# A hybrid-mixer and routed-expert kernel: the last batch's input in the first one's place, the first weight splits in one go, register loads moved into TensorE's idle time, and helper work moved to GpSimd

## The chip, the cores and the metric

The program runs on one core of one Trainium2 chip. The metric is device time in microseconds (us) for one execution; the kernel before was timed three times. The engines are named as in the profile: PE is TensorE (PEld its weight loads), DVE is VectorE, ACT is ScalarE, POOL is GpSimd, SP is SyncE, which issues most of the DMAs. A "q" behind an engine's name (PEldq, ACTq, DVEq, SPq) is that engine's instruction sequencer.

## What is computed

```python
x = L0_attn_x                                   # (4 batches, 512 tokens, 512 features)
h = _layernorm(x) * (1 + ca) + sa               # ca, sa, ga, cb, sb, gb come from silu(c) @ wmod
x = x + ga * _L0_attn_ref(h, ...)               # mixer: causal depthwise conv, B, C, delta products, a scan
h = _layernorm(x) * (1 + cb) + sb
...
logits = x_flat @ w_router.T                    # 2 experts, the token goes to the better one
top_idx = jnp.argmax(probs, axis=-1)
h = jnp.einsum('nd,ehd->enh', x_flat, w_fc)     # 512 -> 2048
a = jnp.square(jnp.where(h >= 0, h, 0.5 * h))
expert_out = jnp.einsum('enh,edh->end', a, w_proj)
out = jnp.einsum('end,en->nd', expert_out, mask * top_weight[None, :])
x = x + gb * out
```

## The kernel before

**Stages.** The program has two large stages. In the first, the mixer, the four batches (`b` = 0 to 3) go one after the other through layernorm, transposes, convolution, scan and output product, and give `res`, the rows after the mixer. For each batch the router's margin is worked out (`margin_products`, `newton2`, `margins`), the tokens of the two experts are counted (`prefix` on PE, `ranks` on DVE), and each block of 128 tokens is permuted on PE (`permuted_block`) and written into the sorted array `XSfull` at a row number that is known only at run time (`place`, from the front for one expert and from the back for the other). In the second stage, the experts, the sorted rows are 17 blocks of 128, in five units of 4, 4, 4, 3 and 2 blocks, and the hidden width is cut into 8 blocks (`hb`). For each unit PE makes the first product (`first_fc` for units 0 and 1 of block 0, else `fc`), DVE and ACT make the square, and PE makes the second product (`proj`).

**High and low parts.** All expert products are made in three passes of a reduced format. A tile is split into a high part (a rounded copy, made by ACT: `Whi`, `XShi`, `ahi`) and a low part (full minus high, made by DVE or POOL: `Wlo`, `XSlo`, `alo`). The weights' two tiles have 8 chunks of 512 columns: chunks 0 to 3 serve the first product, chunks 4 to 7 the second.

**Order of the work.** Every engine's order is written out by hand, and engines wait for each other by semaphores. Around the change it is this. When batch 3 has its mask, PE makes `prefix(3)`, loads four run-time row numbers and expert picks (`load_unit(0)`, `load_unit(1)`), makes the high-high pass of unit 0 (`first_fc(0, (0,))`), the four permuted blocks of batch 3, the other two passes of unit 0, the three of unit 1, seven more register loads, and then `proj(0, 0, 0)`, the first product of the second kind. From there on PE has work until almost the end. DVE makes `ranks(3)`, `permutations(3)`, `low_rows(0)` (the low part of unit 0's rows), `lows(range(4))` (the low weights 0 to 3), `assign_rest` (which rows units 2 to 4 hold), `low_rows(1)`, and then for unit 0 `place_from_back` of blocks 0 and 1, `twice`, `place_from_back` of blocks 2 and 3, and `low`. ACT makes `place(2, ...)`, `high_rows(0)`, `high_rows(1)`, `place(3, (0, 1))`, the high weights 4 to 7 (`split_first(range(4, CH))`) and the first unit's job.

**Memory.** The fourth batch's input `x3` has a place of its own, in the bytes of the high weights 4 to 7; these weights can only be split when batch 3's residual has been read. The inputs of batches 0 to 2 lie in a ring of three places, `x_in`, in the bytes of `XShi`. SP loads `x3` when the third modulation row is done (`s_mm`), and behind it in its queue stand the store of the scaled router rows (`wd_dram`), their four broadcast loads `bc`, which `margin_products(0)` reads, and the router's sums.

**Register loads.** `value_load` reads one number from memory into a register of the engine. In the trace it is three instructions of the sequencer: `TENSOR_LOAD`, `FUSED_REGOPS`, `SEQ_ASSERT`.

Of the kernel before, what the change touches and what calls it, by code (L numbers as in the profile page):

```python
# [104 lines left out]
def build(nc, x, cT, wmod, wx, win, wout, conv_w, conv_b, A_log, Dvec, router_rows, wffn, out):  # L105
    with ExitStack() as ctx:
# [296 lines left out]
        s_early = sem("first_units_assigned")  # L403
        s_unit = sem("units_assigned")
# [30 lines left out]
        def _(sp):  # L435
# [3 lines left out]
            def load_x(b):  # L439
                sp.dma_start(x_in[:, b] if b < XRING else x3[:, :, :], x[b]).then_inc(s_x[b], 16)  # L440
# [22 lines left out]
            sp.wait_ge(s_mm, 4)  # L463
# [49 lines left out]
        def _(pool):  # L513
# [52 lines left out]

            def low(hb, c):
                pool.wait_ge(s_whi, CH * hb + c + 1)
                pool.tensor_tensor(Wlo[:, hb % 2, c, :], raw[:, c, :], Whi[:, hb % 2, c, :].bitcast(F32),  # L569
                                   ALU.subtract).then_inc(s_wlo, 1)  # L570

            for b in range(NB):
# [3 lines left out]
                positions(b)  # L576
                if b == NB - 1:

                    pool.wait_ge(s_wlo, CH // 2)
# [80 lines left out]
        def _(act):  # L660
# [96 lines left out]

            def place(b, js=range(TJ)):
# [107 lines left out]
            def high_rows(u):  # L866
                start_row = act.value_load(startI[0:1, u:u + 1], min_val=0, max_val=ROWS - P * UNITS[u])
                for k in range(KT):
                    act.activation(XShi[:, k, bass.ds(start_row, P * UNITS[u])], XSfull[:, k, bass.ds(start_row, P * UNITS[u])],
                                   ACT.Copy).then_inc(s_xhi, 1)  # L870


            act.wait_ge(s_early, 2)
            act.wait_ge(s_e0, KT * TJ * (NB - 1))
# [48 lines left out]
            for u in range(NU):  # L923
                if u == 0:
                    job(0, 0, 0, ((place, (NB - 1, (2, 3))),))
# [3 lines left out]
                else:  # L929
                    job(0, 0, u, ((high_rows, (u + 1,)),) if u + 1 < NU else ())  # L930
# [22 lines left out]
        def _(pe):  # L953
# [114 lines left out]

            def prefix(b):
# [5 lines left out]
            def permuted_block(b, j):  # L1075
# [16 lines left out]
                mm.then_inc(s_pz, 1)  # L1092

# [22 lines left out]
            for b in range(NB):  # L1116
# [45 lines left out]
                if b == 0:  # L1162
                    delta_product(2)
                prefix(b)
# [108 lines left out]
            start_row, pick = [], []  # L1273

            def load_unit(u):
                start_row.append(pe.value_load(startI[0:1, u:u + 1], min_val=0, max_val=ROWS - P * UNITS[u]))
                pick.append(pe.value_load(pickI[0:1, u:u + 1], min_val=0, max_val=2))


            pe.wait_ge(s_early, 2)  # L1280
            load_unit(0)
            load_unit(1)
# [4 lines left out]
            for j in range(TJ):  # L1287
                permuted_block(NB - 1, j)
            first_fc(0, (1, 2))
# [25 lines left out]
        def _(dve):  # L1315
# [166 lines left out]
            def prepare_rest():  # L1482


                own.link(dve.tensor_scalar(rows_in_front[:, :], ends[:, 1:2], float(P), None, ALU.mult))
                own.mark(dve.tensor_scalar(basis[:, 0:NU - 2], basis[:, 0:NU - 2], rows_in_front[:, 0:1], None, ALU.add))
                own.link(dve.tensor_scalar(limits[:, :], blkF[:, 0:LEFT], rows_in_front[:, 0:1], None, ALU.add))
# [316 lines left out]
```

## Time and profile before

| | |
|---|---|
| timed runs | 545.67, 542.83, 544.35 us; median 544.35 us |
| the profiled execution | 547.68 us, its span 545.9 us |
| granted TensorE clock, mean over the span | 0.958 |
| busy: PE, DVE, ACT, POOL | 92%, 63%, 48%, 29% |
| first matmul of `proj(0, 0, 0)` | at 167.32 us of the span |

The span runs from the first to the last instruction. The chain of work that ended last is followed back from the last instruction. A granted clock of 1.00 is 2.4 GHz, 0.50 is 1.2 GHz. Times in rows are microseconds from the start of the span, followed by the length of the group.

### The profile page before, as it was taken

Reading aid. Unit: us, or ns where it says so; the run is one execution under the profiler, and the core shown is the slowest. Engines: PE = TensorE matmul, PEld = TensorE weight load, DVE = VectorE, ACT = ScalarE, POOL = GpSimd, SP = SyncE. Lnnn points to the kernel's source line nnn. Section 1 sums busy time; section 2 is a strip of 40 time slices with the busy share of each in tenths; the row PEclk is TensorE's granted clock in tenths of the full one; section 3 lists DMA queues with packets and bytes.
Section 4 is the critical chain, followed back from the end, with each engine's and each line's share of the span. In section 5 each row is a group of like instructions: output and inputs, shape, how many; then the busy total and the mean of one; then the engine's idle time right before and its main releaser. Section 6 shows DMA issues by size and latency. Waiting matters only on the chain.

```text
span 545.9 us, 7958 instructions
## 1 busy us (share of the span) xinstructions
PE 502.0 (92%) x2408; PEld 392.8 (72%) x2408; DVE 345.7 (63%) x730; ACT 259.4 (48%) x524; POOL 158.4 (29%) x204
## 2 busy tenths in 40 slices
PE   7899789987397999999999999999999999999990
PEld 1464365736276888898888888888888888988880
DVE  4579999699998575454445354545454534668781
ACT  1774295956785633443443354344345334433220
POOL 1100021122243510330150033034004304868673
PEclk9899969998697999999999999999999999999995
DMA  8931242220051004130022022002102300468692
GB/s 294 424 133 57 103 152 77 79 77 2 1 162 72 4 3 156 30 126 2 1 79 79 1 78 80 1 1 94 64 1 78 118 1 6 117 112 182 78 167 98
DMA packets 15730, 46.31 MB, mean 85 GB/s; under 512 B 5223, under 2 KB 5223, under 8 KB 12344
## 3 DMA queue, kind: packets, MB, share of 16 engines
q1 hardware_dynamic: 10600, 34.71, 17.9%
q0 software_dynamic: 5072, 10.79, 9.6%
q8 instruction: 41, 0.67, 0.5%
q14 instruction: 17, 0.14, 0.1%
HBM read 37.30 MB, written 8.71 MB: 84 GB/s over the span
## 4 chain that ended last, share of the span: by engine, by line
PE 75%; DVE 13%; ACT 4%; issue 3%; DMA 1%; ACTq 1%; POOL 1%; DVEq 0%; SPq 0%; POOLq 0%
PE bank L1232 34%; PE bank L1201 32%; DVE xc L1359 3%; ACT XSfull L777 2%; DVE st L1404 1%; DVE st L1341 1%; DMA x_in<-x 1%; PE bank L1030 1%; PE bank L1038 1%; DVE res L1397 1%; PE bank L1063 1%; PE bank L1006 1%; DVE eabs L1421 1%; PE bank L1067 1%; DVE hs L1387 1%
## 5 line engine op out<-in xcount | busy, mean ns | idle before, releaser
L569 POOL TENSOR_TENSOR Wlo<-raw,Whi (+1 forms) x60 | 76.6, 1307 | 228.0 <-ACT Whi L921 219.9
L1656 DVE TENSOR_TENSOR acc<-acc,bank 128x512 f32<-128x512 f32 x110 | 74.8, 687 | 57.2 <-PE bank L1232 57.2
L1232 PE MATMUL bank<-Whi,ahi 128*128 128x512 f32 x268 | 105.5, 394 | 4.3 <-DVE alo L1646 4.3
L1640 DVE TENSOR_TENSOR twice_h<-twice_h,bank 128x512 f32<-128x512 f32 (+2 forms) x80 | 48.2, 605 | 95.6 <-ACT twice_h L892 95.5
L1201 PE MATMUL bank<-XShi,Wlo 128*128 x304 | 108.1, 356 | 0.0
L1201 PE MATMUL bank<-XSlo,Whi 128*128 x304 | 108.0, 355 | 0.0
L1201 PE MATMUL bank<-XShi,Whi 128*128 x304 | 108.0, 355 | 0.0
L1232 PE MATMUL bank<-Wlo,ahi 128*128 128x512 f32 x268 | 105.5, 394 | 0.0
L1232 PE MATMUL bank<-Whi,alo 128*128 128x512 f32 x268 | 105.3, 393 | 0.0
L901 ACT ACTIVATE ahi<-twice_h 128x512 fp32r<-128x512 f32 (+2 forms) x78 | 44.6, 572 | 120.0 <-PE bank L1232 119.9
L892 ACT ACTIVATE twice_h<-bank 128x512 f32<-128x512 f32 (+2 forms) x78 | 41.4, 533 | 86.9 <-PE bank L1201 76.2
L1201 PEld LDWEIGHTS bank<-XSlo,Whi 128*128 128x128 f32 x304 | 57.3, 189 | 7.5
L1201 PEld LDWEIGHTS bank<-XShi,Whi 128*128 128x128 f32 x304 | 57.3, 189 | 7.5
L1201 PEld LDWEIGHTS bank<-XShi,Wlo 128*128 128x128 f32 x304 | 57.3, 188 | 6.8
L1232 PEld LDWEIGHTS bank<-Whi,ahi 128*128 128x128 f32 x268 | 51.0, 190 | 14.9 <-issue 4.7
L1232 PEld LDWEIGHTS bank<-Whi,alo 128*128 128x128 f32 x268 | 50.9, 190 | 10.8
L1232 PEld LDWEIGHTS bank<-Wlo,ahi 128*128 128x128 f32 x268 | 50.9, 190 | 10.2
L1646 DVE TENSOR_TENSOR alo<-a_full,ahi 128x512 fp32r<-128x512 f32 (+2 forms) x78 | 45.4, 612 | 0.0
L902 ACT ACTIVATE a_full<-twice_h 128x512 f32<-128x512 f32 (+2 forms) x78 | 43.3, 556 | 0.0
L1359 DVE SCALAR_TENSOR_TENSOR xc<-hT,cw,xc 128x512 f32<-128x512 f32 x48 | 33.6, 742 | 2.5 <-ACT xc L703 2.2
L777 ACT ACTIVATE XSfull<-bank,cols 128x128 f32 (+1 forms) x64 | 24.1, 460 | 20.0 <-PE bank L1091 17.7
L921 ACT ACTIVATE Whi<-raw 128x512 fp32r<-128x512 f32 x56 | 30.5, 616 | 0.0
(201 smaller groups left out, 570.1 us busy)
## 6 DMA issues: line engine op xcount, KB each, us to landing
raw<-wffn SPq DMA_DIRECT2D x16, 1024.0 KB, 5.1
wm<-wmod SPq DMA_DIRECT2D x6, 1024.0 KB, 12.8
out<-res SPq DMA_DIRECT2D x4, 1024.0 KB, 4.5
x_in<-x SPq DMA_DIRECT2D x3, 1024.0 KB, 12.4
ga_bc<-ga_rows SPq DMA_DIRECT2D x4, 256.0 KB, 3.7
x<-x SPq DMA_DIRECT2D x1, 1024.0 KB, 5.1
bc<-router_rows_scaled SPq DMA_DIRECT2D x4, 256.0 KB, 3.5
wx_sb<-wx SPq DMA_DIRECT2D x1, 514.0 KB, 8.6
```

The costliest lines, as they stand in the source:

```text
L569: pool.tensor_tensor(Wlo[:, hb % 2, c, :], raw[:, c, :], Whi[:, hb % 2, c, :].bitcast(F32), ALU.subtract).then_inc(s_wlo, 1)
L777: act.activation(XSfull[:, k, bass.ds(first, P)], place_bank[b][j][:, P * k:P * k + P], ACT.Identity, bias=cols[:, 4, k, b:b + 1], scale=c ...
L892: act.activation(twice_h[:, m, 0:w], hP[(par + u) % 2][m][:, 0:w], ACT.Relu).then_inc(s_relu[m], 1)
L901: act.activation(ahi[:, m, 0:w], twice_h[:, m, 0:w], ACT.Square, scale=0.5).then_inc(s_ah[m], 1)
L902: act.activation(a_full[:, m, 0:w], twice_h[:, m, 0:w], ACT.Square, scale=0.5).then_inc(s_af[m], 1)
L921: act.activation(Whi[:, 1 - par, c, :], raw[:, c, :], ACT.Copy).then_inc(s_whi, 1)
L1201: mm = pe.matmul(hP[(par + u) % 2][m][:, c0:c1], W[wp][:, par, 2 * e + k // 2, o:o + P], XS[xp][:, k, bass.ds(start_row[u] + c0, c1 - c0)] ...
L1232: mm = pe.matmul(yP[bank_of[s]][:, :], ahl[ap][:, m, P * s:P * s + P], W[wp][:, par, 4 + 2 * experts[s] + m, :], start=(m == 0 and n == 0) ...
L1359: ins = dve.scalar_tensor_tensor(xc[:, b % 2, k, :], hT[b % 2][:, k, tap:tap + L], cw[:, k, tap:tap + 1], xc[:, b % 2, k, :], ALU.mult, AL ...
L1640: dve.tensor_tensor(twice_h[:, m, 0:w], twice_h[:, m, 0:w], hP[(par + u) % 2][m][:, 0:w], ALU.add).then_inc(s_q2[m], 1)
L1646: dve.tensor_tensor(alo[:, m, 0:w], a_full[:, m, 0:w], ahi[:, m, 0:w].bitcast(F32), ALU.subtract).then_inc(s_al2[m], 1)
L1656: dve.tensor_tensor(acc[:, n, :], acc[:, n, :], yP[s][:, :], ALU.add).then_inc(s_yu, 1)
```

## The change

The fourth batch is loaded into ring place 0 after batch 0's residual has been read. ACT splits all eight first weights in one go before `place(2, ...)`. The low weights 0 to 3 go from DVE to POOL, ahead of POOL's scatter DMAs of batch 2; the low weights 4 to 7 stay on POOL but wait for `low_rows(1)`. `prepare_rest` (four small operations) goes from DVE to POOL. PE loads the registers of units 0 and 1 ahead of `prefix(3)`, followed by three matmuls whose result is not used (`keep_rate`), and those of units 2 to 4 ahead of the second and third pass of unit 0. ACT and DVE load row numbers earlier. ACT makes the rank guess `guess2(3)` after block 2 of batch 2 instead of after block 1, and three blocks of batch 3 instead of two ahead of unit 0's job. The top weights and the count of batch 3 move from unit 0 to unit 1 on DVE.

```diff
-        x3 = at("x3", [P, TJ, DM], F32, o_whi + ZB)
-
         def x_row(b, j):
-            return x_in[:, b, j, :] if b < XRING else x3[:, j, :]
+            return x_in[:, b % XRING, j, :]
...
-            sp.wait_ge(s_mm, 4)
+            sp.wait_ge(s_x2, TJ)
             load_x(3)
             sp.wait_ge(s_wdr, 1)
             sp.dma_start(wd_dram, wd_row[:, :]).then_inc(s_wds, 16)
...
+            def prepare_rest():
+                pool.wait_ge(s_early, 2)
+                own.link(pool.tensor_scalar(rows_in_front[:, :], ends[:, 1:2], float(P), None, ALU.mult))
...
+                pool.tensor_scalar(limits[:, :], limits[:, :], -1.0, float(TOK), ALU.mult, ALU.add).then_inc(s_limits, 1)
...
+                if b == NB - 2:
+                    prepare_rest()
+
+                    pool.wait_ge(s_x2, TJ * (NB - 1) + 1)
+                    pool.wait_ge(s_pb, 2 * NB)
+                    pool.wait_ge(s_cv, KT * NB)
+                    for c in range(CH // 2):
+                        low(0, c)
                 if b == NB - 1:
 
+                    pool.wait_ge(s_xlo, KT * 2)
                     pool.wait_ge(s_wlo, CH // 2)
                     for c in range(CH // 2, CH):
                         low(0, c)
...
-            split_first(range(4))
-            place(2, (0, 1))
+            split_first(range(CH))
+            place(2, (0, 1, 2))
             guess2(3)
-            place(2, (2, 3))
...
             act.wait_ge(s_early, 2)
+            first_rows = [first_row(u) for u in range(2)]
+            place(2, (3,))
...
-            high_rows(0)
-            high_rows(1)
+            act.wait_ge(s_x2, TJ * NB)
+            high_rows(0, first_rows[0])
+            high_rows(1, first_rows[1])
             margin_exp(3)
-            place(NB - 1, (0, 1))
-
-            act.wait_ge(s_x2, TJ * NB)
-            split_first(range(4, CH))
+            place(NB - 1, (0, 1, 2))
...
+            def keep_rate(b, count):
+
+                pe.wait_ge(s_q, TJ * b + 2)
+                pe.wait_ge(s_x2, TJ * (b + 1))
+                for n in range(count):
+                    pe.matmul(pO[1][:, :], ident[:, :], wout_sb[:, :], start=True, stop=True)
...
+                if b == NB - 1:
+
+                    pe.wait_ge(s_early, 2)
+                    load_unit(0)
+                    load_unit(1)
+                    keep_rate(b, 3)
                 prefix(b)
...
             first_fc(0, (0,))
             for j in range(TJ):
                 permuted_block(NB - 1, j)
-            first_fc(0, (1, 2))
-
-            pe.wait_ge(s_x2, TJ * NB)
-            first_fc(1, (0, 1, 2))
             pe.wait_ge(s_unit, 2)
             for u in range(2, NU):
                 load_unit(u)
             pick.append(pe.value_load(pickI[0:1, NU:NU + 1], min_val=0, max_val=2))
+            first_fc(0, (1, 2))
+
+            pe.wait_ge(s_x2, TJ * NB)
+            first_fc(1, (0, 1, 2))
...
-                    if b == NB - 1:
-                        prepare_rest()
...
+            first_rows = [first_row(u) for u in range(2)]
             ranks(NB - 1)
             permutations(NB - 1)
-            low_rows(0)
-            lows(range(4))
             assign_rest()
-            low_rows(1)
+            dve.wait_ge(s_off, NB)
+            low_rows(0, first_rows[0])
+            first = [first_place(j) for j in range(2)]
+            low_rows(1, first_rows[1])
+            first += [first_place(j) for j in range(2, TJ)]
...
-                if u == 0:
+                if u == 1:
                     own.link(dve.tensor_scalar(n0f[:, :], run[:, :], -1.0, float(TOK), ALU.mult, ALU.add))
```

On PE, between the permuted blocks of batch 2 (`bank<-perm,z`) and the prefix counts of batch 3 (`bank<-m,before` and `bank<-m,ones`), the kernel before has nothing, and the register loads of units 0 and 1 follow the counts (`startI` holds row numbers, `pickI` expert picks):

```order
L1091 MATMUL bank<-perm,z_71 128x128 x8
L1072 MATMUL bank<-m_140,before 128x4
L1073 MATMUL bank<-m_140,ones 128x4
L1276 TENSOR_LOAD startI
L1276 ISA x2
L1277 TENSOR_LOAD pickI
L1277 ISA x2
```

In the changed kernel the same place reads:

```order
L1118 MATMUL bank<-perm,z_71 128x128 x8
L1124 TENSOR_LOAD startI
L1124 ISA x2
L1125 TENSOR_LOAD pickI
L1125 ISA x2
L1124 TENSOR_LOAD startI
L1124 ISA x2
L1125 TENSOR_LOAD pickI
L1125 ISA x2
L1094 MATMUL bank<-wout_sb,ident 128x512 x3
L1099 MATMUL bank<-m_139,before 128x4
L1100 MATMUL bank<-m_139,ones 128x4
```

The four loads and three new matmuls now stand ahead of the counts, and the first pass of unit 0 follows the counts directly.

Further on in PE's order, the end of unit 1's passes, the seven later loads (the last five rows of them here) and the first row of `proj(0, 0, 0)` stood like this before:

```order
L1180 MATMUL bank<-XShi,Wlo 128x512 x8
L1188 UNCONDITIONAL_BRANCH
L1276 TENSOR_LOAD startI
L1276 ISA x2
L1277 TENSOR_LOAD pickI
L1277 ISA x2
```

and in the changed kernel the seven loads begin right behind the permuted blocks of batch 3 and end in front of unit 0's second pass (`bank<-XSlo,Whi`), of which this is the end:

```order
L1124 TENSOR_LOAD startI
L1124 ISA x2
L1125 TENSOR_LOAD pickI
L1125 ISA x2
L1321 TENSOR_LOAD pickI
L1321 ISA x2
L1225 COMPARE_AND_BRANCH
L1219 ISA
L1219 MATMUL bank<-XSlo,Whi 128x512
```

On DVE, from the permutation masks of batch 3 on (`perm`), the kernel before makes the low rows of unit 0 and the low weights ahead of the assignment of the later units (`begun`, `change`, `assignment`):

```order
L1454 TENSOR_SCALAR perm<-colidx,place_col 128x128 x4
L1619 TENSOR_LOAD startI
L1619 ISA x2
L1622 ISA
L1622 TENSOR_TENSOR XSlo<-XSfull,XShi 128x512
L1622 ISA
L1622 TENSOR_TENSOR XSlo<-XSfull,XShi 128x512
L1622 ISA
L1622 TENSOR_TENSOR XSlo<-XSfull,XShi 128x512
L1622 ISA
L1622 TENSOR_TENSOR XSlo<-XSfull,XShi 128x512
L1527 TENSOR_TENSOR Wlo<-raw,Whi 128x512 x4
```

In the changed kernel:

```order
L1483 TENSOR_SCALAR perm<-colidx,place_col 128x128 x4
L1514 TENSOR_SCALAR begun<-limits,run 128x8
L1515 TENSOR_TENSOR change<-change,begun 128x56
L1517 TENSOR_REDUCE assignment<-change 128x7
L1518 TENSOR_TENSOR startI<-assignment,basis 128x3
L1519 TENSOR_TENSOR pickI<-assignment,basis 128x4
L1639 ISA
L1639 TENSOR_TENSOR XSlo<-XSfull,XShi 128x512
```

The assignment now comes first, the register load is gone from this place, and the four low weights are gone from DVE.

## Rows read from the trace of the kernel before

**Rows 1.** Chain that ended last, in order of time: start, length, what.
```profile
167.32 8.16 PE bank L1232 x24
175.48 5.44 PE bank L1201 x24
```

**Rows 2.** Timeline of PE from batch 3's counts to the first second product.
```profile
145.19 0.59 PE L1072 MATMUL bank<-m,before 128*128 128x4 f32 x2 [5.19 <-DVE m L1435]
...
148.50 3.70 PE L1180 MATMUL bank<-XShi,Whi 128*128 x8 [2.30 <-ACT XShi L869]
152.04 1.91 PE L1091 MATMUL bank<-perm,z 128*128 128x128 f32 x16
153.70 2.07 PE L1180 MATMUL bank<-XSlo,Whi 128*128 x8
...
167.32 0.80 PE L1232 MATMUL bank<-Whi,ahi 128*128 128x512 f32 x1 [4.29 <-DVE alo L1646]
```

**Rows 3.** Timeline of DVE in the same stretch.
```profile
148.83 2.50 DVE L1622 TENSOR_TENSOR XSlo<-XSfull,XShi  x4
151.25 2.49 DVE L1527 TENSOR_TENSOR Wlo<-raw,Whi 128x512 fp32r<-128x512 f32 x4
...
155.18 3.60 DVE L1622 TENSOR_TENSOR XSlo<-XSfull,XShi  x4 [0.54 <-issue]
158.70 1.35 DVE L1633 TENSOR_SCALAR XSfull<-bank,cols 128x128 f32 x4
...
161.56 1.27 DVE L1640 TENSOR_TENSOR twice_h<-twice_h,bank 128x512 f32<-128x512 f32 x2
...
165.61 1.28 DVE L1646 TENSOR_TENSOR alo<-a_full,ahi 128x512 fp32r<-128x512 f32 x2
```

**Rows 4.** Timeline of POOL: the low weights 4 to 7.
```profile
156.64 5.80 POOL L569 TENSOR_TENSOR Wlo<-raw,Whi 128x512 fp32r<-128x512 f32 x4 [8.01 <-ACT Whi L756]
```

**Rows 5.** Timeline of ACT in the same stretch.
```profile
147.05 4.27 ACT L869 ACTIVATE XShi<-XSfull  x8 [0.80 <-ACT XSfull L781]
...
154.47 1.51 ACT L777 ACTIVATE XSfull<-bank,cols 128x128 f32 x4 [0.20 <-ACT XSfull L777]
155.85 2.20 ACT L756 ACTIVATE Whi<-raw 128x512 fp32r<-128x512 f32 x4
157.94 1.09 ACT L892 ACTIVATE twice_h<-bank 128x512 f32<-128x512 f32 x2
```

**Rows 6.** PE's sequencer by line: durations ns min/median/max, first and last start.
```profile
L1276 PEldq TENSOR_LOAD <-startI x2: 297/362/427, 159.2 to 160.6; - x2
...
L1296 PEldq SEQ_ASSERT  x1: 18/18/18, 163.8 to 163.8; - x1
...
L1089 PEldq EVENT_SEMAPHORE  x2: 51/51/51, 150.0 to 150.2; - x2
```

**Rows 7.** One stretch: us, busy PE, PEld, DVE, ACT, POOL, then granted clock, DMA share, GB/s.
```profile
140.00:142.00 2.00, 0.00 (x0) 0.00 (x0) 1.68 (x8) 1.18 (x6) 0.00 (x0) 0.93 0.00 0
```

**Rows 8.** Timeline of PE: three matmuls of full format, 512 columns, two records each.
```profile
61.49 2.74 PE L1048 MATMUL bank<-xc,win_sb 128*128 128x512 f32 x6
```

**Rows 9.** Timeline of SP and DVE around the router rows' broadcast.
```profile
56.48 0.68 DVE L1397 TENSOR_TENSOR res<-bank,x_in 128x512 f32<-128x512 f32 x1
...
61.24 1.74 SPq L470 DMA_DIRECT2D bc<-router_rows_scaled  x4
...
64.35 2.46 DVE L1341 BATCH_NORM_STATS2 st<-x 128x6 f32<-128x512 f32 x4
...
67.48 0.69 DVE L1421 CUSTOM_DVE_ANT_0 eabs<-res,bc 128x512 f32<-128x512 f32 x1
```

**Rows 10.** DMA issues on the page: size, median us from issue to landing.
```profile
x_in<-x SPq DMA_DIRECT2D x3, 1024.0 KB, 12.4
...
x<-x SPq DMA_DIRECT2D x1, 1024.0 KB, 5.1
...
bc<-router_rows_scaled SPq DMA_DIRECT2D x4, 256.0 KB, 3.5
```

More of the change, by code:

```diff
@@ L403, in build @@
         s_early = sem("first_units_assigned")
+        s_limits = sem("limits_ready")
         s_unit = sem("units_assigned")
@@ L439, in load_x @@
             def load_x(b):
-                sp.dma_start(x_in[:, b] if b < XRING else x3[:, :, :], x[b]).then_inc(s_x[b], 16)
+                sp.dma_start(x_in[:, b % XRING], x[b]).then_inc(s_x[b], 16)
             sp.dma_start(c_sb[:, :], cT).then_inc(s_c, 16)
@@ L756, in split_first, with first_row, high_rows @@
                     act.activation(Whi[:, 0, c, :], raw[:, c, :], ACT.Copy).then_inc(s_whi, 1)
+            def first_row(u):
+                return act.value_load(startI[0:1, u:u + 1], min_val=0, max_val=ROWS - P * UNITS[u])
+            def high_rows(u, start_row):
+                for k in range(KT):
+                    act.activation(XShi[:, k, bass.ds(start_row, P * UNITS[u])], XSfull[:, k, bass.ds(start_row, P * UNITS[u])],
+                                   ACT.Copy).then_inc(s_xhi, 1)
             def place(b, js=range(TJ)):
@@ L924, in _ @@
                 if u == 0:
-                    job(0, 0, 0, ((place, (NB - 1, (2, 3))),))
+                    job(0, 0, 0, ((place, (NB - 1, (3,))),))
                     act.wait_ge(s_e0, KT * NBLK)
@@ L929, in _ @@
                 else:
-                    job(0, 0, u, ((high_rows, (u + 1,)),) if u + 1 < NU else ())
+                    job(0, 0, u, ((lambda n: high_rows(n, first_row(n)), (u + 1,)),) if u + 1 < NU else ())
                 if u == 1:
@@ L1092, in permuted_block, with load_unit @@
                 mm.then_inc(s_pz, 1)
+            start_row, pick = [], []
+            def load_unit(u):
+                start_row.append(pe.value_load(startI[0:1, u:u + 1], min_val=0, max_val=ROWS - P * UNITS[u]))
+                pick.append(pe.value_load(pickI[0:1, u:u + 1], min_val=0, max_val=2))
             pe.wait_ge(s_const, 9)
@@ L1480, in assign_first @@
                 dve.tensor_copy(startI[:, 0:2], startf[:, :]).then_inc(s_early, 1)
[L1482 to L1487, printed above, removed]
-                own.link(dve.tensor_scalar(limits[:, :], limits[:, :], -1.0, float(TOK), ALU.mult, ALU.add))
             def assign_rest():
                 dve.wait_ge(s_change, CHANGES)
+                dve.wait_ge(s_limits, 1)
                 own.link(dve.tensor_scalar(begun[:, :], limits[:, :], run[:, 0:1], None, ALU.is_gt))
@@ L1617, in _, with first_row, low_rows @@
                 margins(b)
-            def low_rows(u):
-                start_row = dve.value_load(startI[0:1, u:u + 1], min_val=0, max_val=ROWS - P * UNITS[u])
+            def first_row(u):
+                return dve.value_load(startI[0:1, u:u + 1], min_val=0, max_val=ROWS - P * UNITS[u])
+            def low_rows(u, start_row):
                 for k in range(KT):
@@ L1623, in low_rows, with first_place, place_from_back @@
                                       XShi[:, k, bass.ds(start_row, P * UNITS[u])].bitcast(F32), ALU.subtract).then_inc(s_xlo, 1)
-            def place_from_back(j):
+            def first_place(j):
+                return dve.value_load(offI[0:1, (NB - 1) % 2, j:j + 1], min_val=0, max_val=P * (TJ * (NB - 1) + j))
+            def place_from_back(j, first):
                 b = NB - 1
                 n = TJ * b + j
-                first = dve.value_load(offI[0:1, b % 2, j:j + 1], min_val=0, max_val=P * n)
                 dve.wait_ge(s_e0, KT * (n + 1))
@@ L1711, in _ @@
                 if u == 0:
-                    place_from_back(0)
-                    place_from_back(1)
+                    place_from_back(0, first[0])
+                    place_from_back(1, first[1])
                 twice(0, 0, u)
                 if u == 0:
-                    place_from_back(2)
-                    place_from_back(3)
+                    place_from_back(2, first[2])
+                    place_from_back(3, first[3])
                 elif u + 1 < NU:
-                    low_rows(u + 1)
+                    if u == 1:
+                        dve.wait_ge(s_unit, 2)
+                    low_rows(u + 1, first_row(u + 1))
                 if u > 0:
```

20 lines of the change are left out of this document (4 added, 16 removed).

## Prediction

> **What bounds the kernel now.** I read the chain of waits first. It is mixed up to 167.32 us of the span and is PE alone from there: the second and first products of the experts follow each other without a gap [rows 1] until the last few microseconds. The change adds and removes no matmul behind that point. So its worth is the moment at which `proj(0, 0, 0)` starts, and the rate at which PE then runs.
>
> Next I read the timeline of PE in front of that moment. The last pass of unit 1 was done at about 163.0, and PE then sat idle for 4.29 us, until DVE had made `alo` [rows 2]. In the idle time the granted clock fell: the first 24 matmuls of `proj` took 8.16 us, the next 24, of the same size, 5.44 us [rows 1]. The reader is to see two separate losses there, 4.29 us of idle time and 2.72 us of slow clock.
>
> Then I followed back what `alo` waited for, on DVE and ACT. DVE is busy almost without a gap from 148.83: low rows 2.50, low weights 2.49, assignment, low rows 3.60, two blocks from the back from 158.70, `twice` 1.27, two more blocks, `alo` [rows 3]. The 3.60 is the same work as the 2.50; it ran long while POOL made its low weights, from 156.64 [rows 3, 4]. ACT had unit 0's `h` waiting while it split the weights 4 to 7 (2.20 us), and made the first half of the square at 157.94 [rows 5]. DVE is thus the engine that sets `proj`'s start, with ACT close behind.
>
> **The change, part by part.**
>
> *DVE.* The four low weights (2.49) leave it. The register load in front of `low_rows(1)` (0.54 of idle time) is hidden, and the 1.10 by which `low_rows(1)` ran long is avoided, since POOL now waits for it [rows 3]. Counting nothing for `prepare_rest`, the masks are done at 148.8 as before. The assignment takes about 0.9 (from the end of the low weights at 153.74 to 155.18, less the 0.54), so 149.8. Two times 2.50 of low rows end at 154.8, where they ended at 158.78 before. Two blocks of 1.35 with a gap of 0.2 end at 157.7. DVE is then some 4 us earlier, and waits for ACT.
>
> *PE, the loads.* This is the part that costs. Seven loads took from 159.2 to 163.8, so 4.6 us, 0.66 each [rows 6], and before they lay beside unit 1's matmuls and the idle time. Now they stand in front of unit 0's second pass. PE's sequencer had passed the waits of the permuted blocks at 150.2 [rows 6], well ahead of the matmuls, which ended at about 153.9 [rows 2]. Its condition, the assignment, is met at 149.8. So the loads run from 150.3 to 154.9. With 0.4 for the branch (as from the end of `alo`, 166.89, to 167.32) the second pass starts at 155.3 instead of 153.70 [rows 2]: 1.6 us later. Unit 0's two remaining passes take 3.7 (from 153.70 to 157.4 before, and 16/24 of 5.44), so its `h` is complete at 159.0.
>
> *ACT.* The weight split leaves this place and goes to a wait ahead of `place(2, ...)`; it was on the way of `twice_h` only through its 2.20 us, of which one more block of 1.51 takes the place [rows 5]. From the complete `h` at 159.0: the last half of the first operation, 0.55, ends at 159.65.
>
> *The sum.* From 159.65 on DVE: half of `twice` 0.65, two blocks 2.9 with their gap, `alo` 1.28 [rows 3], branch 0.42: 164.9. ACT has one block (1.7 with its gap) and four squares of 0.56 ahead of the second `alo`, which gives 163.6, within that. So `proj` starts at about 165.0 instead of 167.32: **2.3 us** earlier. Unit 1's three passes (5.44) run from 159.0 to 164.5. PE's idle time ahead of `proj` shrinks from 4.29 to 0.5 us, and with it goes the reason for the slow clock: **2.7 us** [rows 1]. Together 5.0 us.
>
> *Against it.* PE is done with the permuted blocks at 152.2 to 153.9 and now idles until 155.3, up to 3.1 us. Before, the clock was at 0.93 in the mean of a stretch in which PE did nothing, so it fell inside it, some 2 us after the last matmul of that place [rows 7]. If it falls in the new gap too, unit 0's passes run at 1.2 GHz for a while. The bounds are 0 and 3.7 us (all 16 matmuls at half rate); a pass of eight at the lower level took 3.70 against 2.07 [rows 2], so one slow pass costs 1.6. I take 0.8, the middle of none and one.
>
> The Trainium skill speaks on this against the change, in "TensorE: Matmul & The Clock Gate", Part 4: it says that a transpose does not count as PE being busy in the way a matmul does, so the 1.9 us of permuted blocks ahead of the gap would not hold the clock up. The trace agrees as far as it goes, since the blocks of batch 2 did not keep the clock from falling. By that rule one slow pass, 1.6, would be taken in full, and the sum would be 3.4 us.
>
> *`keep_rate` and the first loads.* Four loads (2.6 by the rate of the seven) and three matmuls now stand ahead of `prefix(3)`, in PE's 5.19 us of idle time before 145.19 [rows 2]. PE's last matmul ahead of it ended at 140.0; the sequencer is a little ahead, so I put the loads' end at 142.1. Three matmuls of full format took 2.74 us at full rate [rows 8], so 2.7, or 5.4 at half. At full rate they end at 144.8, ahead of the mask; at half rate at 147.5, and the counts, which DVE used at about 147.2 before, come up to 1.5 us late. DVE has 4 us to spare later, but the loads' condition moves too. I take 0 and keep 1.5. What the matmuls may bring, a first pass at full rate (1.6 us), hides behind the seven loads.
>
> *ACT's loads.* Three in a row ahead of the last block of batch 2, about 1.9; `high_rows(0)` then starts close to its 147.05 [rows 5]. No gain, and up to 0.5 late; PE's first pass is covered by the loads. `guess2(3)` moves behind a block of 1.5 and its copy; DVE's four margin products give it about that time.
>
> *The fourth input.* It is issued after batch 0's last residual (56.48 + 0.68), 57.2 [rows 9], and lands 5.1 us later [rows 10], 62.3; its first reader stands at 64.35 [rows 9]. Behind it in SP's queue are the router rows' store and the four `bc` loads, issued at 61.24. If the store ends with the input, `bc` is issued at 62.4 instead, the last of the four at 63.7, and lands 3.5 later, at 67.2. Its reader stands at 67.48 [rows 9, 10]. Cost 0, with a slack that is nearly gone.
>
> "DMA: Bandwidth & Descriptors" of the Trainium skill, Queues, rings and completion order, says that each DMA engine takes a queue's descriptors in ring order. No stretch of this trace shows a small store behind a large load; by the rule it waits for the load, which the case above already assumes.
>
> *POOL.* Its four low weights (5.80 [rows 4]) run from about 134.6 to 140.4; batch 2's scatters come after and end near 145.5, when the mask arrives. The second four run from 154.8 to 160.6, and `proj` needs them at 165. Nothing here is on the path.
>
> **The rivals.** First, the clock takes the gain: it falls in the gap of the loads and again ahead of `proj`, or the counts come late by 1.5. Then `proj` starts 0 to 2 us earlier and partly at half rate: 0.3 to 2.6 us gained, 541.8 to 544.0. For it speaks the 3.1 us gap; against it, that unit 1's passes run right into `proj`. The change then does not do what it says for TensorE's waits: one is removed and one made. Chance 0.22.
>
> Second, more is gained: the seven loads overlap with the permuted blocks so that the second pass still starts at 153.7. That gives 1.6 more, 6.6 us, 537.8. Against it stand the 4.6 us. Chance 0.12.
>
> Third, slower: the fourth input lands late. The loads into `x_in` had a median of 12.4 us to landing, in a full queue [rows 10]. With 12.4 it would land at 69.6, `bc` at 74.5 instead of 67.2, and DVE would stand 7.0 us from 67.48, in a stretch where the counts on PE wait for DVE. With the 4.2 us gained elsewhere that is 547.1. It decides against the change from a landing later than about 9 us after issue. DMA has nothing else to do at that time, so 0.10, other losses included.
>
> **How the numbers follow.** The forecast (0.56) is 5.0 less 0.8, 4.2 us. The profiled execution took 547.68, so its counterpart is 543.5; the median of the three runs is 544.35, and I forecast 540.1, its own range 538.6 to 541.5. The runs shown differ by 2.8 us, so 0.5% (2.7 us) is about what a measurement can tell from no change. To hold 8 in 10 the range goes up into the first rival and down to the second: 537.0 to 544.6. Faster by over 0.5%: the forecast, the second rival, nothing of the first: 0.68. Within: 0.22. Slower: 0.10.
>
> **What would show it.** In the changed kernel: seven register loads on PE's sequencer ending near 155, unit 0's second pass right after them, DVE's second low rows at 2.5 us and over by 155; `proj(0, 0, 0)` near 165 with an idle time under 1 us and 24 matmuls in 5.4 us; the input's landing near 62.3 and no wait of DVE for `bc`. I am wrong if PE's idle time only moves ahead of unit 0's second pass and brings the slow clock with it, or if anything before 145 comes late.

## The result, and the profile after

The changed kernel took 552.84 us in the median of 4 runs (551.69 to 553.85), against 543.85 for the kernel before in the same comparison: a ratio of 1.0147, 95% interval 1.0115 to 1.018. It is slower, where 540.1 was forecast. The profiled execution took 553.41, with a span of 551.6.

The chain that ended last, of the changed kernel, two stretches: start, length, what (L1271 is `proj`, L1240 `fc`). A `...` in a view marks rows left out.
```profile
167.02 5.78 PE bank L1271 x24
172.80 5.44 PE bank L1240 x24
...
189.99 2.90 issue
192.89 0.69 DVE alo L1665
193.58 0.42 issue
194.00 7.65 PE bank L1271 x24
```

These answer to [rows 1]. `proj(0, 0, 0)` starts at 167.02, 0.3 earlier, and its 24 matmuls take 5.78 where they took 8.16: 2.4 gained, as the prediction's second term said. But 27 us later there is a break that [rows 1] do not have. The loss is there: TensorE stands still, and then runs 24 matmuls in 7.65 instead of 5.44 (its granted clock from 194 to 198 is 0.50). The rows around it, by engine:

Timelines of POOL, DVE, ACT and PE of the changed kernel, 176 to 194 us (L604 and L608 are the scatters, L578 the low weights, L1665 `alo`).
```profile
176.15 1.02 POOL L604 DMA_INDIRECT sorted_rows<-meta,posI  x1 [16.80 <-issue]
...
181.36 1.11 POOL L608 DMA_INDIRECT sorted_rows<-gap,gapI  x1 [0.30 <-issue]
182.49 9.92 POOL L578 TENSOR_TENSOR Wlo<-raw,Whi  x8
...
184.33 9.24 DVE L1665 TENSOR_TENSOR alo<-a_full,ahi 128x512 fp32r<-128x512 f32 x2
...
184.84 2.18 ACT L941 ACTIVATE Whi<-raw 128x512 fp32r<-128x512 f32 x4
...
194.00 0.80 PE L1271 MATMUL bank<-Whi,ahi 128*128 128x512 f32 x1 [6.13 <-DVE alo L1665]
```

The two `alo` instructions of unit 2 took 9.24 us together, where those of unit 0 took 1.28 [rows 3]. One of them alone lasted 8.6 us. It ended at 192.97, 0.6 after POOL's eight low weights (192.41), so it ran only when they were through. The view of the tile `alo` (count, ns min/median/max):
```profile
L1665 DVE TENSOR_TENSOR alo<-a_full,ahi x2: 679/4660/8642, 184.3 to 192.9; 128x512 fp32r<-128x512 f32 x2
```

The two spans add up: 0.3 and 2.4 gained, 6.1 of idle time and 2.2 of slow clock lost, which is 5.6 us; the spans differ by 5.7 (551.6 less 545.9). The medians differ by more, since the profiled execution of before (547.68) was itself 3.8 above its median.

Why the eight run in one piece shows in POOL's first row: the scatters of batch 3 start at 176.15. In the kernel before they started at 168.26, and the low weights of block 1 came in two fours, at 177.66 and 188.52, with the `alo` of unit 2 (187.00) between them. Timelines of POOL and DVE of the kernel before (L569 are the low weights, L1646 `alo`).
```profile
168.26 1.02 POOL L586 DMA_INDIRECT sorted_rows<-meta,posI  x1 [5.82 <-issue]
...
177.66 5.05 POOL L569 TENSOR_TENSOR Wlo<-raw,Whi  x4 [3.16 <-ACT Whi L921]
188.52 5.24 POOL L569 TENSOR_TENSOR Wlo<-raw,Whi  x4 [5.81 <-ACT Whi L921]
```
```profile
187.00 1.33 DVE L1646 TENSOR_TENSOR alo<-a_full,ahi 128x512 fp32r<-128x512 f32 x2
```
There POOL waited 5.81 us ahead of the second four, for ACT's second half of the high weights. In the changed kernel POOL comes so late that this half is being made (184.84) while it works on the first four, and it goes straight on.

The scatters wait for the weights of batch 3 and the count (`n0f`, `gapI`, `top_weight(3)`), and the change moves these on VectorE from unit 0 to unit 1, the last line of the diff.

The transition itself, for [rows 2] and [rows 3]. Timelines of PE and DVE of the changed kernel.
```profile
140.76 5.46 PE L1094 MATMUL bank<-wout_sb,ident 128*128 128x512 f32 x6 [3.12 <-DVE q L1450]
...
149.69 1.91 PE L1118 MATMUL bank<-perm,z 128*128 128x128 f32 x16
154.36 3.77 PE L1219 MATMUL bank<-XSlo,Whi 128*128 x8 [2.76 <-DVE XSlo L1639]
```
```profile
142.19 0.17 DVE L1464 TENSOR_SCALAR m<-lg 128x4 f32<-128x4 f32 x1
...
146.91 0.16 DVE L1470 TENSOR_TENSOR place_col<-cand,bank 128x4 f32<-128x4 f32 x1 [2.36 <-PE bank L1100]
...
149.38 4.91 DVE L1639 TENSOR_TENSOR XSlo<-XSfull,XShi  x8
...
160.51 0.69 DVE L1659 TENSOR_TENSOR twice_h<-twice_h,bank 128x512 f32<-128x512 f32 x1 [3.35 <-ACT twice_h L912]
```
The three matmuls of `keep_rate` ran at half rate (5.46 where [rows 8] have 2.74, granted clock 0.50 from 142 to 146), held the counts back, and VectorE stood 2.36 us. The low rows run undisturbed (4.91 for both units). TensorE stood 2.76 us ahead of unit 0's second pass, whose eight matmuls took 3.77.

### The profile page after: what moved, and what is told of

The parts are those of the page before. It is cut to its first block, busy times and chain, and to the rows that moved or that the text cites. A ratio compares the mean times of both kernels' runs of the same rounds, so it can differ in the third digit from the quotient of the medians.

```text
span 551.6 us, 7975 instructions
## 1 busy us (share of the span) xinstructions
PE 506.8 (92%) x2414; PEld 394.1 (71%) x2414; DVE 349.1 (63%) x722; ACT 260.0 (47%) x524; POOL 163.8 (30%) x212
## 4 chain that ended last, share of the span: by engine, by line
PE 72%; DVE 18%; issue 4%; ACT 2%; DMA 1%; DVEq 1%; POOL 1%; SPq 0%; ACTq 0%; POOLq 0%
PE bank L1271 34%; PE bank L1240 32%; DVE xc L1388 4%; PE bank L1219 2%; DVE st L1433 2%; DVE res L1426 2%; DVE st L1370 1%; DMA x_in<-x 1%; DVE eabs L1450 1%; PE bank L1094 1%; DVE hs L1416 1%; PE bank L1050 1%; PE bank L1068 1%; PE bank L1058 1%; PE bank L981 1%
## 5 line engine op out<-in xcount | busy, mean ns | idle before, releaser
L578 POOL TENSOR_TENSOR Wlo<-raw,Whi (+1 forms) x64 | 80.4, 1292 | 224.0 <-ACT Whi L941 217.9
L1271 PE MATMUL bank<-Whi,ahi 128*128 128x512 f32 x268 | 105.5, 394 | 6.5 <-DVE alo L1665 6.5
L1240 PE MATMUL bank<-XShi,Wlo 128*128 x304 | 108.1, 356 | 0.0
L1240 PE MATMUL bank<-XSlo,Whi 128*128 x304 | 108.1, 355 | 0.0
L1240 PE MATMUL bank<-XShi,Whi 128*128 x304 | 108.1, 355 | 0.0
L1271 PE MATMUL bank<-Wlo,ahi 128*128 128x512 f32 x268 | 105.3, 393 | 0.0
L1271 PE MATMUL bank<-Whi,alo 128*128 128x512 f32 x268 | 105.2, 392 | 0.0
L1271 PEld LDWEIGHTS bank<-Whi,ahi 128*128 128x128 f32 x268 | 50.9, 190 | 17.4 <-issue 7.2
L1240 PEld LDWEIGHTS bank<-XShi,Whi 128*128 128x128 f32 x304 | 57.3, 189 | 7.5
L1240 PEld LDWEIGHTS bank<-XSlo,Whi 128*128 128x128 f32 x304 | 57.3, 189 | 7.5
L1240 PEld LDWEIGHTS bank<-XShi,Wlo 128*128 128x128 f32 x304 | 57.3, 189 | 6.9
L1271 PEld LDWEIGHTS bank<-Whi,alo 128*128 128x128 f32 x268 | 50.8, 189 | 10.8
L1271 PEld LDWEIGHTS bank<-Wlo,ahi 128*128 128x128 f32 x268 | 50.8, 190 | 10.1
L1665 DVE TENSOR_TENSOR alo<-a_full,ahi 128x512 fp32r<-128x512 f32 (+2 forms) x78 | 53.3, 714 | 0.0
L941 ACT ACTIVATE Whi<-raw 128x512 fp32r<-128x512 f32 x56 | 30.5, 617 | 0.0
```

The source lines that it names most:

```text
L941: act.activation(Whi[:, 1 - par, c, :], raw[:, c, :], ACT.Copy).then_inc(s_whi, 1)
L1240: mm = pe.matmul(hP[(par + u) % 2][m][:, c0:c1], W[wp][:, par, 2 * e + k // 2, o:o + P], XS[xp][:, k, bass.ds(start_row[u] + c0, c1 - c0)] ...
L1271: mm = pe.matmul(yP[bank_of[s]][:, :], ahl[ap][:, m, P * s:P * s + P], W[wp][:, par, 4 + 2 * experts[s] + m, :], start=(m == 0 and n == 0) ...
L1665: dve.tensor_tensor(alo[:, m, 0:w], a_full[:, m, 0:w], ahi[:, m, 0:w].bitcast(F32), ALU.subtract).then_inc(s_al2[m], 1)
```

## The experiments

The theory that I began with, called A in the expectations: the moved lines make the scatters late, the low weights of block 1 then run eight in a row, VectorE's `alo` does not run beside them, and TensorE waits for it. Against it stood that the transition makes the loss (B), that only the whole change's timing does (C), and that what costs is being late, not the overlap (D).

Each kernel is a few lines away from one of the two, and each is compared, by the ratio of the times, with the kernel before on the same chip. "The changed kernel, count back" is the base of most.

**1. The count put back.**
```
-                if u == 1:
+                if u == 0:
                     own.link(dve.tensor_scalar(n0f[:, :], run[:, :], ...
```


> Theory A (the move of the count and of batch 3's top weights from unit 0 to unit 1 costs the time: GpSimd's scatters become late, its eight low weights of block 1 then run back to back, and VectorE's `alo` of unit 2 is held): with that code back in unit 0, the scatters leave by about 169, GpSimd's low weights of block 1 run as two groups of four (each some 5.0 us), the longest `alo` is again near 0.7 us, TensorE's idle 6.1 us ahead of `proj(0,0,1)`'s successor and its slow 24 matmuls (7.65 instead of 5.44 us) are gone: 553 minus 8.3 is about 544.5 us. Rival B (the loss is made in the transition by the three extra matmuls and the earlier register loads): about 552, and the idle time stays.

Measured: 545.06 us against 545.97, ratio 0.9984 (0.9959 to 1.001). The loss is gone. Timeline of POOL of this kernel:
```profile
162.74 1.02 POOL L604 DMA_INDIRECT sorted_rows<-meta,posI  x1 [6.06 <-issue]
...
169.75 5.06 POOL L578 TENSOR_TENSOR Wlo<-raw,Whi  x4 [0.77 <-ACT Whi L941]
180.61 5.22 POOL L578 TENSOR_TENSOR Wlo<-raw,Whi  x4 [5.81 <-ACT Whi L941]
```
Two fours again, and the longest `alo` of the whole run is 694 ns:
```profile
L1665 DVE TENSOR_TENSOR alo<-a_full,ahi x78: 416/685/694, 160.1 to 515.2; 128x512 fp32r<-128x512 f32 x48, 128x384 fp32r<-128x384 f32 x16, 128x256 fp32r<-128x256 f32 x14
```

**2. Only the count moved, in the kernel before** (the same line, the other way round).

> The kernel before, with nothing but the count and batch 3's top weights moved from unit 0 to unit 1. Theory A: the scatters come 8 to 9 us later, at about 179 to 185; GpSimd starts block 1's low weights at about 185, ScalarE's second half of the split (187.5) is there in time for them to follow without a pause, VectorE's `alo` of unit 2 (187.0) is held to about 195: 7 to 9 us more than before, about 552. Rival B: no change, 544. Rival C (the count alone is harmless; only the earlier schedule of the changed kernel makes the eight run together): within 1 us of before.

Measured: 553.9 us against 545.97, ratio 1.0159 (1.0129 to 1.0188). Timeline of POOL, and tile `alo`:
```profile
183.77 1.10 POOL L590 DMA_INDIRECT sorted_rows<-gap,gapI  x1 [0.30 <-issue]
184.88 9.92 POOL L569 TENSOR_TENSOR Wlo<-raw,Whi  x8
```
```profile
L1646 DVE TENSOR_TENSOR alo<-a_full,ahi x2: 679/4269/7859, 187.5 to 195.3; 128x512 fp32r<-128x512 f32 x2
```
One line of the diff makes the whole loss, in either kernel. Rivals B and C fall.

**3. The count in unit 1, but POOL's low weights wait.**
```
+            pool.wait_ge(s_al2[HM - 1], 3)
             with pool.Fori(1, NHB - 1) as hb:
```


> The changed kernel with the count still in unit 1, but GpSimd's low weights of block 1 wait until VectorE's `alo` of unit 2 is made (about 185.7), so that they start 3 us later than in the changed kernel and still run eight in a row. Theory A in its narrow form (it is the overlap with that one VectorE operation, not that GpSimd is late): `alo` takes 0.7 us again, TensorE's idle 6.1 us goes, about 545; the `alo` of unit 3 (about 194) may be held for the last 1 to 2 us of GpSimd's stretch, which ends at about 195.6. Rival D (what costs is that block 1's low weights or the scatters are late): more than 553, since they are later still.

Measured: 547.64 us against 545.97, ratio 1.0032 (1.0008 to 1.0056). The `alo` pair of unit 2 took 1.33 us again, so being late is not what makes the loss of 8 us, and D falls for that. About 545 was expected; 1.7 us over the kernel before are left, and TensorE's timeline has a wait that the kernel before lacks, 1.78 us at 189.41, ahead of unit 4's first product, which needs the low rows of unit 4. For the run of eight now lay over the low rows of unit 4 (I had expected unit 3's `alo`, which was not hit). Timelines of POOL and DVE:
```profile
182.51 10.74 POOL L578 TENSOR_TENSOR Wlo<-raw,Whi  x8 [3.98 <-ACT Whi L942]
```
```profile
180.39 1.33 DVE L1666 TENSOR_TENSOR alo<-a_full,ahi 128x512 fp32r<-128x512 f32 x2
...
185.25 5.62 DVE L1640 TENSOR_TENSOR XSlo<-XSfull,XShi  x4 [0.21 <-ACT XShi L782]
```
Four instructions that take 1.42 alone took 5.62, some 1.5 each (1336 to 1514 ns): VectorE and GpSimd took turns. Nothing was held for 8 us, although eight low weights ran in a row. That did not fit the theory, and the next run was made for it.

**4. Scatters early, the eight held back until they lie over `alo`** (base: count back).
```
+            pool.wait_ge(s_xlo, KT * 4)
             with pool.Fori(1, NHB - 1) as hb:
```


> The changed kernel with the count and batch 3's top weights back in unit 0 (so the scatters leave early), but with GpSimd's low weights of block 1 held until VectorE's low rows of unit 3 are made (about 176.6), so that ScalarE's second half of the split (from about 180.6) is there before the first four are done. Theory A, the run of eight over VectorE's `alo` of unit 2 (about 179.1): `alo` is held to about 186.6, TensorE idles some 5 to 6 us and the time is 550 to 553. If it is the lateness of the scatters or of batch 3's top weights that costs (rival D), there is nothing late here: about 545.

Measured: 545.51 us against 544.57, ratio 1.001 (0.9989 to 1.0031). Timelines of POOL and DVE:
```profile
180.53 11.48 POOL L578 TENSOR_TENSOR Wlo<-raw,Whi  x8 [8.20 <-DVE XSlo L1640]
```
```profile
182.43 2.88 DVE L1666 TENSOR_TENSOR alo<-a_full,ahi 128x512 fp32r<-128x512 f32 x2
```
`alo` began 1.9 us into the eight, as in the changed kernel (1.8), and took 2.88 us instead of 9.24. My theory A, as put down for this run, is refuted: an unbroken run of eight over `alo` is not enough. What the two slow kernels have and this one has not is a scatter directly ahead of the eight.

**5. As 4, with the last scatter held as well.**
```
             pool.wait_ge(s_n0, 1)
+            pool.wait_ge(s_xlo, KT * 4)
             pool.indirect_dma_start(out=meta_dram, ... gapI ...
```


> As the kernel that held block 1's low weights until the low rows of unit 3, but with the last scatter (`gap`) held with them, so that the low weights follow directly behind a scatter, as they do in the changed kernel. Theory E (VectorE's operation is held to the end only in a run of low weights that begins directly behind a scatter, without a pause on GpSimd): the `alo` of unit 2 (about 182.4) is held for 6 to 9 us, to the end of the eight, and the time is 550 to 553. Rival F (what holds it is something else that the changed kernel and the count moved alone have in common, such as the four scatters of batch 3 or SyncE's five loads of the sorted rows, which come just then): `alo` takes 1.2 to 1.8 us again and the time is about 545.

Measured: 554.59 us against 546.09, ratio 1.0154 (1.0107 to 1.0202). Timelines of POOL, DVE and PE:
```profile
180.54 0.95 POOL L609 DMA_INDIRECT sorted_rows<-gap,gapI  x1 [9.44 <-DVE XSlo L1640]
181.51 9.90 POOL L578 TENSOR_TENSOR Wlo<-raw,Whi  x8
```
```profile
182.46 10.11 DVE L1666 TENSOR_TENSOR alo<-a_full,ahi 128x512 fp32r<-128x512 f32 x2
```
```profile
192.99 0.79 PE L1272 MATMUL bank<-Whi,ahi 128*128 128x512 f32 x1 [6.99 <-DVE alo L1666]
```

**6. The changed kernel, with a pause between scatter and low weights.**
```
+            pool.wait_ge(s_yu, FIRST[1] + 2)
             with pool.Fori(1, NHB - 1) as hb:
```


> The changed kernel as it is, count in unit 1, scatters late, but GpSimd waits between its last scatter (which ends at about 182.5) and the low weights of block 1 for the second of VectorE's sums of unit 1 (about 183.1): a pause of 0.6 to 1 us. Theory E: the `alo` of unit 2 (about 184.3) now takes turns with the low weights (1.2 to 1.8 us each instead of 8.6), TensorE's idle 6.1 us goes, and the time is about 545 to 548. Rival F: `alo` is held to the end again, which comes 0.6 us later: 553 to 554.

Measured: 546.71 us against 546.09, ratio 1.0001 (0.9973 to 1.0028). Timelines of POOL and DVE:
```profile
180.65 1.10 POOL L608 DMA_INDIRECT sorted_rows<-gap,gapI  x1 [0.30 <-issue]
183.12 11.66 POOL L578 TENSOR_TENSOR Wlo<-raw,Whi  x8 [1.37 <-DVE acc L1674]
```
```profile
183.61 3.05 DVE L1666 TENSOR_TENSOR alo<-a_full,ahi 128x512 fp32r<-128x512 f32 x2
```
Runs 4 and 5 differ by where one scatter stands, and by 1.4% in their ratios. Run 6 leaves the scatters as late as the changed kernel has them and adds a pause of 1.37 us: the loss is gone. Rival F falls on both sides.

**7. As 5, with a pause in the middle of the eight.** Ahead of the fifth low weight POOL waits for `s_al2[HM - 1]` to reach 3.

> As the kernel with the `gap` scatter directly ahead of block 1's low weights, but the last four of the eight wait for VectorE's `alo` of unit 2. If the hold lasts as long as GpSimd's unbroken run behind a scatter (Theory E), the `alo` that starts at about 182.5 is held to the end of the first four (about 186.5), some 4 us instead of 9.5; behind the pause the last four take turns with the low rows of unit 3 (some 1.5 us each). TensorE, which stood 7.0 us before its next product, stands 1 to 2 us: the time is 546 to 548. If the hold does not depend on the run's length but on the scatter alone, the `alo` is held for over 5 us or not at all.

Measured: 547.33 us against 544.42, ratio 1.0046 (1.0014 to 1.0079). Timelines of POOL, DVE and PE:
```profile
177.27 0.96 POOL L609 DMA_INDIRECT sorted_rows<-gap,gapI  x1 [9.43 <-DVE XSlo L1644]
178.25 5.02 POOL L578 TENSOR_TENSOR Wlo<-raw,Whi 128x512 fp32r<-128x512 f32 x4
184.51 5.54 POOL L578 TENSOR_TENSOR Wlo<-raw,Whi 128x512 fp32r<-128x512 f32 x4 [1.23 <-DVE alo L1670]
```
```profile
179.18 5.24 DVE L1670 TENSOR_TENSOR alo<-a_full,ahi 128x512 fp32r<-128x512 f32 x2
```
```profile
184.86 0.80 PE L1276 MATMUL bank<-Whi,ahi 128*128 128x512 f32 x1 [2.13 <-DVE alo L1670]
```
The hold is as long as what is left of the unbroken run: 4.64 us of one `alo`, to the end of the four. Behind the pause the last four take turns with the low rows (of unit 4). Here the eight are written out and not in POOL's loop, so the loop is not what makes the hold.

**8. As 5, with a small copy between scatter and low weights.** `pool.tensor_copy(posF, pos)` behind the scatter.

> As the kernel with the `gap` scatter directly ahead of block 1's low weights, with one small copy on GpSimd (128x4, `pos` to `posF`, some 0.2 to 0.3 us) between the scatter and the first low weight, and no wait that makes GpSimd pause. If it takes a pause of GpSimd to end the hold (Theory E as it stands), the `alo` of unit 2 is held to the end of the eight again and the time is near 554. If any other instruction behind the scatter ends it, `alo` takes turns (1.2 to 1.8 us each) and the time is 545 to 547.

Measured: 551.43 us against 543.39, ratio 1.0116 (1.0063 to 1.0169). Timelines of POOL and DVE:
```profile
181.30 0.20 POOL L613 COPY posF<-pos 128x4 f32<-128x4 f32 x1
181.46 9.88 POOL L578 TENSOR_TENSOR Wlo<-raw,Whi  x8
```
```profile
182.26 10.23 DVE L1668 TENSOR_TENSOR alo<-a_full,ahi 128x512 fp32r<-128x512 f32 x2
```
Another instruction does not end the hold. Of what was tried, only a pause of POOL did.

**9 to 12. The other parts of the change.** Run 9: the kernel before with only the fourth input loaded over the first.

> The kernel before with only the fourth batch of inputs loaded over the first (and its load held until batch 0's residuals are made). As predicted, it costs nothing: within 0.5 us of before. Rival: the clock of 0.50 between 70 and 80 us, which the kernel before shows and three of four kernels with the changed load do not, comes from where that load stands: then this kernel shows the clock back at 1.00 by 74 and is about 2.5 us faster.

Run 10: count back, without `keep_rate`.

> The changed kernel with the count back in unit 0, and without the three matmuls ahead of `prefix(3)`. If they are in the way of `prefix(3)` (VectorE's idle 2.36 us in the changed kernel), up to 2 us faster than with them (about 543); if the clock that they keep up is worth as much, the same (545 to the kernel with the count put back, within 0.7 us).

Run 11: count back, the seven register loads behind `first_fc(1, ...)` again.

> The changed kernel with the count back in unit 0, and TensorE's seven register loads behind `first_fc(1, ...)` again, the three matmuls kept. The seven loads take about 4.6 us behind the permutation, where TensorE waits some 2.8 us for the low rows: unit 0's second pass starts up to 1.8 us earlier, but the loads now stand ahead of `proj(0,0,0)`, where before they were hidden behind its wait for `alo`. I expect the same time as with the count put back alone, within 1 us.

Run 12: both of these.

> The changed kernel with the count back in unit 0, without the three extra matmuls ahead of `prefix(3)`, and with TensorE's seven register loads behind `first_fc(1, ...)` again. If the extra matmuls cost what VectorE's idle 2.36 us ahead of `ranks(3)` shows, and the loads make the clock fall ahead of unit 0's second pass, then `first_fc(0, (0,))` starts about 2 us earlier than in the changed kernel: about 542, 2 to 3 us under the kernel that has only the count put back. If both are hidden (rival), the two kernels are equal within 0.5 us.

Measured:

| run | us | before | ratio, 95% interval |
|---|---|---|---|
| 9, load only | 543.63 | 544.57 | 0.9985 (0.9959 to 1.0011) |
| 10, no `keep_rate` | 543.89 | 544.57 | 0.9986 (0.9963 to 1.0009) |
| 11, loads back | 542.48 | 544.57 | 0.9954 (0.993 to 0.9978) |
| 12, both | 543.74 | 545.97 | 0.9967 (0.9946 to 0.9988) |

The fourth input costs nothing, as predicted. Whether it lifts the clock between 70 and 80 us stays open: that clock was 0.83 in run 9's profile and 0.50 in the profile of before, but run 9's time does not differ measurably. `keep_rate` makes no difference that these runs can tell. Run 11 is the best kernel of the study, 0.46% under the kernel before. That was a miss: I had expected the time of run 1 within 1 us, and for run 12 either 542 or that time within 0.5. Run 11's timeline of PE shows that unit 0's second pass follows the permutation without a gap:
```profile
150.95 2.65 PE L1118 MATMUL bank<-perm,z 128*128 128x128 f32 x16
153.35 2.09 PE L1219 MATMUL bank<-XSlo,Whi 128*128 x8
```
and the loads, now ahead of `proj`, cost TensorE next to nothing there: it stood 1.16 us, for `alo`. Against the kernel with only the count put back, which was compared on another chip, run 11 is lower by 0.3% with overlapping intervals, so the part of the loads in the gain is likely and not shown. Run 10, on run 11's chip, is 1.4 us slower at the medians, but differs from it in two things, the loads and `keep_rate`.

## Why the prediction was wrong

**The step that failed** is the one on POOL, "Nothing here is on the path", together with the one in the first part, "The change adds and removes no matmul behind that point. So its worth is the moment at which `proj(0, 0, 0)` starts, and the rate at which PE then runs." I followed POOL's low weights of block 0 and its scatters of batch 2, and did not follow the four instructions that the diff moves from unit 0 to unit 1. They are 0.7 us of VectorE's time and look free. But POOL's five scatters wait for them, the low weights of block 1 stand behind the scatters, and in the kernel before these low weights left the `alo` of unit 2 between their two halves. With the scatters 8 us later they ran over it, directly behind a scatter. None of my three rivals had this; the one that ended slower, with 0.10, was the input's landing, and it did not happen: `bc` was issued at 62.16 (62.4 predicted) and its reader stood at 67.60 (before 67.48).

What it costs is shown by run 2 alone: 1.59% of 545.97, 8.7 us (7.9 between the medians). The profile of the changed kernel has it as 6.1 us of idle time and 2.2 of slow clock.

**The rest of the sum**, with the count put back, was 4.2 us in the forecast and measured 0.9 (a loss of 0.5 to a gain of 2.2, run 1). Two terms:

*The clock ahead of `proj`*, 2.7 us. Right in kind, and 1.6 to 2.4 in size: in the profiles of all ten kernels that have the new transition and of the changed kernel the first 24 matmuls took 5.73 to 5.78, and 7.40 to 8.16 in the three that have the old one.

*`proj` 2.3 us earlier, less 0.8 of slow clock.* Too large. From VectorE's mask of batch 3 to the start of `proj(0, 0, 0)` the profiles show:

| | mask | `proj` | between |
|---|---|---|---|
| before | 144.96 | 167.32 | 22.4 |
| run 2, old transition | 144.85 | 167.21 | 22.4 |
| run 9, old transition | 143.84 | 165.10 | 21.3 |
| changed kernel | 142.19 | 167.02 | 24.8 |
| runs 1, 3, 4, 5, 6, 7, 8 | | | 20.4, 21.3, 22.4, 22.3, 22.5, 20.4, 21.9 |
| run 11, loads back | 142.97 | 163.85 | 20.9 |
| run 10, no `keep_rate` | 142.78 | 165.03 | 22.3 |
| run 12, both | 142.91 | 164.11 | 21.2 |

The middle of the seven is 21.9, half a microsecond under the kernel before and not 2.3 or 1.5. What stood in the way in these seven is a term that the prediction put at "No gain, and up to 0.5 late": ACT's three register loads ahead of the last block of batch 2. It priced them at 1.9 us; the profiles show ACT idle for 2.75 to 3.59 there, and for 0.49 in the kernel before. In the changed kernel:
```profile
143.68 1.51 ACT L803 ACTIVATE XSfull<-bank,cols 128x128 f32 x4 [3.24 <-issue]
...
146.11 4.27 ACT L781 ACTIVATE XShi<-XSfull  x8 [0.17 <-ACT XSfull L807]
```
ACT's high rows (L781) begin 2.3 to 4.4 us after the mask in the seven, and 2.1 in the kernel before, so the earlier mask is lost on them; TensorE's first pass waited for them in all eight. From the start of the high rows on, `proj` comes 18.1 to 18.6 us later in all seven, against 20.3 before: that part, 1.7 to 2.2 us, came near the forecast 2.3 less 0.8. These are readings of one profile each, and no run moves ACT's loads alone.

The gap ahead of unit 0's second pass came as forecast, and in the changed kernel's own profile it was worse: `keep_rate` at half rate made the counts late, the case of "up to 1.5 us late" that I had kept as a bound and counted as 0; VectorE stood 2.36 us. The second pass and the third (3.77 and 3.24) then ran slow, 3.0 us above full rate where I had taken 0.8. The rule of the Trainium skill that I weighed there ("TensorE: Matmul & The Clock Gate", Part 4, transposes don't hold the clock up) would have the pass behind the gap run slow. The changed kernel's profile agrees, with 3.77 (granted clock 0.50 from 154.4 to 158). Run 1's does not: behind the same sixteen transposes and a gap of 2.73 its pass took 2.16, and the clock stayed at 1.00. Nor do the seven other profiles with the loads in this place, with 2.09 to 2.23 behind gaps of 1.20 to 2.71.

These two terms together, 2.4 and 0.5, would give 2.9 us. Run 1 measured 0.9, and its interval ends at 2.2. Where the other 2 us went is not settled; single executions of that kernel spread from 540.97 to 547.72, and one profile each does not resolve it. One likely part, not shown: the forecast took its losses from a single execution that was 3.8 us above its kernel's median. Run 9 has the old transition too, in a profile 1.2 above its median, and there the second low rows took 2.50 and not 3.60, TensorE stood 2.21 ahead of `proj` and not 4.29, and the 24 matmuls took 7.40 and not 8.16. From the mask to the end of these 24 that makes 28.7 us in run 9 and 30.5 in the kernel before, against 27.6 in the middle of the seven: a gain of 1.0 by the one and 2.9 by the other.

**Right** were the low rows undisturbed by POOL (4.91 for eight), the idle time ahead of `proj` at 0.37 (0.5 predicted), and the fourth input at no cost, with `bc` issued as late as forecast.

## What to carry to other kernels

A move of a few cheap instructions has to be followed through the queues of every engine that waits for them: who waits, what stands behind the waiter, and beside what it will now run. Two engines that were kept apart by nothing but their order in time (here GpSimd's low weights and VectorE's `alo`) are a schedule that no wait protects; look in the profile for the longest execution of an instruction, not only its mean. And where GpSimd goes from a DMA that it issues straight into long elementwise work, a wait that makes it pause ahead of that work (1.37 us here) saved the whole loss.

## What the runs showed of the hardware

In these traces a VectorE instruction with both inputs in SBUF and GpSimd's elementwise subtraction, where they met, did not run at once. In most overlaps they took turns: low rows of 0.41 us took 1.5 (run 3), `alo` of 0.68 took 1.2 and 1.8 (run 4), near the 1.25 to 1.3 of one low weight. The Trainium skill says so in "SBUF — State Buffer", SBUF: two separate sides: such a VectorE instruction and a GpSimd instruction that reads SBUF exclude each other, and the one that starts first has the ports for its whole instruction. The turns agree with it.

The hold does not. When GpSimd went from a scatter into the low weights without a pause, VectorE's instruction was held through all that were left of the run, 7859 to 9630 ns in four kernels with eight (the changed kernel, runs 2, 5, 8) and 4643 ns with four (run 7), and VectorE got no turn between them. After a pause of GpSimd of 1.37, 3.98 or 8.20 us it got one after each (runs 6, 3, 4). Why the scatter and the missing pause do this, the runs don't show. Another kind of DMA was not tried. Pauses of 0.77 and 0.74 us behind the scatter stand in runs 1 and 10, but VectorE's next such instructions met only the last of the four low weights there, and decide nothing.

Loading a register took longer where several loads followed each other on ACT: `TENSOR_LOAD` took 637 to 902 ns in the changed kernel and 278 to 283 in the kernel before, where they stood apart. The DMA engines, idle at 140 to 142 us in the kernel before, were fully busy then in the changed one, and TensorE's own four loads ended at 140.6; which of these makes the loads longer was not tested.
